# GpSimd issues two of the four transfers that bring a unit's probability blocks back

## What is computed

```python
xn = layernorm(x, ln_x_g, ln_x_b);  ln = layernorm(latents, ln_l_g, ln_l_b)
q = ln @ Wq
kv = concatenate([xn @ Wkv, ln @ Wkv], axis=1)
sim = einsum('bhid,bhjd->bhij', rmsnorm(q, qn_g) * scale, rmsnorm(k, kn_g))
attn = softmax(sim)                       # over 1024 context rows and 64 latents
out = einsum('bhij,bhjd->bhid', attn, v)  # then @ Wout + bout
```

## Time and profile before

| | |
|---|---|
| median of 3 runs | 220.82 us (219.22 to 222.07) |
| profiled execution | 220.61 us |
| its span | 218.8 us |
| TensorE's mean granted clock | 0.997 of full speed |
| busy: TensorE, weight loads, VectorE, ScalarE, GpSimd | 210.0, 179.2, 158.3, 142.1, 83.2 us |
| by the six stores (`p_spread<-xnh_room` and `<-xnl_room`) | 512 KB each |
| by the 24 read-backs | 128 KB each |

### The profile page before, as it was taken

How to read it: one execution, slowest core, us unless ns; L and a number is a source line. 1 busy time by engine, 2 the same in 40 slices (tenths; PEclk the granted TensorE clock), 3 DMA queues, 4 the chain that set the end, 5 groups by cost and what they waited for, 6 DMA issues and landing times.

```text
span 218.8 us, 4012 instructions
## 1 busy us (share of the span) xinstructions
PE 210.0 (96%) x1338; PEld 179.2 (82%) x1338; DVE 158.3 (72%) x355; ACT 142.1 (65%) x316; POOL 83.2 (38%) x135
## 2 busy tenths in 40 slices
PE   8899999999999999999999999999799999999984
PEld 7566878887787988889898988978588998899873
DVE  3799999998978989898886758876477651613531
ACT  3777798979985968776676595945566563315060
POOL 4388887872393939355160500012101200000400
PEclk9999999999999999999999999999999999999998
DMA  5491127110000232331514899435754580000000
GB/s 169 150 313 39 52 52 263 48 51 0 2 25 0 97 100 96 96 140 55 186 61 139 284 415 322 116 136 192 240 192 169 197 142 12 4 0 0 0 3 24
DMA packets 22820, 25.07 MB, mean 115 GB/s; under 512 B 7656, under 2 KB 20112, under 8 KB 22544
## 3 DMA queue, kind: packets, MB, share of 16 engines
q1 hardware_dynamic: 21384, 20.10, 29.6%
q0 software_dynamic: 864, 3.15, 3.7%
q10 hardware_dynamic: 552, 1.58, 2.1%
HBM read 18.65 MB, written 5.90 MB: 112 GB/s over the span
## 4 chain that ended last, share of the span: by engine, by line
PE 57%; DVE 13%; ACT 9%; issue 7%; DMA 6%; POOL 6%; SPq 1%; ACTq 0%; POOLq 0%; DVEq 0%
PE banks L1611 11%; PE banks L1505 8%; PE banks L1436 7%; PE banks L1545 6%; PE banks L1819 5%; PE banks L1661 3%; DVE small L1089 3%; DMA xnl_room<-p_spread 2%; DVE sk L1101 2%; DMA raw<-in_ctx 2%; PE banks L1625 2%; ACT sp L759 2%; PE banks L1626 2%; PE banks L1668 2%; PE banks L1548 2%
## 5 line engine op out<-in xcount | busy, mean ns | idle before, releaser
L607 POOL TENSOR_TENSOR small<-small 128x16 f32<-128x16 f32 x7 | 20.4, 2915 | 27.4 <-DVE small L1096 27.4
L720 ACT ACTIVATE sk<-banks 128x512 f32<-128x512 f32 x36 | 20.8, 602 | 11.7 <-PE banks L1505 11.1
L1089 DVE TENSOR_REDUCE small<-sk 128x8 f32<-128x512 f32 x36 | 23.5, 679 | 3.5 <-ACT sk L720 3.5
L1101 DVE TENSOR_TENSOR sk<-banks,small 128x512 f32<-128x512 f32 x36 | 23.0, 680 | 2.7 <-POOL small L607 2.4
L759 ACT ACTIVATE sp<-sp,small 128x1088 f32<-128x1088 f32 x16 | 19.2, 1203 | 7.4 <-DVE small L1120 6.9
L1611 PE MATMUL banks<-xnh,pth 128*128 128x256 f32 x80 | 23.6, 295 | 0.0
L1505 PE MATMUL banks<-wkh,xth 128*128 128x512 f32 x68 | 22.7, 415 | 0.6 <-ACT xth L700 0.5
L1611 PE MATMUL banks<-xnh,ptl 128*128 128x256 f32 x80 | 22.6, 283 | 0.0
L1611 PE MATMUL banks<-xnl,pth 128*128 128x256 f32 x80 | 22.6, 283 | 0.0
L1120 DVE CUSTOM_DVE_ANT_0 sp<-banks,mbias 128x1088 f32<-128x1088 f32 x16 | 20.5, 1284 | 2.0 <-PE banks L1548 2.0
L1505 PE MATMUL banks<-wkl,xth 128*128 128x512 f32 x68 | 21.4, 396 | 0.3 <-DVE wkl L1187 0.3
(11 more groups left out here) (227 smaller groups left out, 538.3 us busy)
## 6 DMA issues: line engine op xcount, KB each, us to landing
knT<-in_L_attn_qkv_kernel SPq DMA_DIRECT2D x1, 3072.0 KB, 12.1
spread<-knT SPq DMA_DIRECT2D x5, 512.0 KB, 2.6
knT<-spread SPq DMA_DIRECT2D x20, 128.0 KB, 2.9
raw<-in_ctx SPq DMA_DIRECT2D x16, 128.0 KB, 2.4
p_spread<-xnh_room POOLq DMA_DIRECT2D x3, 512.0 KB, 3.1
xnh_room<-p_spread SPq DMA_DIRECT2D x12, 128.0 KB, 2.8
p_spread<-xnl_room POOLq DMA_DIRECT2D x3, 512.0 KB, 3.4
xnl_room<-p_spread SPq DMA_DIRECT2D x12, 128.0 KB, 3.0
```

The costliest lines, as they stand in the source:

```text
L607: nc.gpsimd.tensor_tensor(rn[:, i % 2, :], n2[:, i % 2, :], mhalf, ALU.pow).then_inc(rnp_ready, 1)
L720: nc.scalar.activation(sk[:, i % 2, h * 512:(h + 1) * 512], banks[:, k_bank(i, h), :], ACT.Square).then_inc(sq_ready, 1)
L1089: mark(nc.vector.tensor_reduce(n2[:, i % 2, 8 * h:8 * h + 8], sk[:, i % 2, h * 512:(h + 1) * 512].rearrange("p (h d) -> p h d", d=DH), AX. ...
L1101: nc.vector.tensor_tensor(sk[:, i % 2, h * 512:(h + 1) * 512].rearrange("p (h d) -> p h d", d=DH), banks[:, k_bank(i, h), :].rearrange("p ...
```

## The change

SP issues the first two reads of each unit (rows 0 to 63 of `p_back`). The other two are issued by GpSimd, in `store_blocks(u)` behind the store of the same unit, after a wait for that store and, from n = 2, for `ptl_ready`, as SP has it. Each of GpSimd's twelve reads has a semaphore of its own, `pq_by_pool[n][c]`. ScalarE waits for both of them beside `pq_landed`, whose count per unit falls from 64 to 32. The lines behind the new line 296 are one further down (on ScalarE, nine to ten).

```diff
--- before.py
+++ after.py
@@ -293,6 +293,7 @@
         mh_ps = sem("mh_ps")
         ph_half = sem("ph_half")
         pb_stored = [sem(f"pb_stored{n}") for n in range(UNITS - SPREAD)]
+        pq_by_pool = [[sem(f"pq_by_pool{n}_{c}") for c in range(2)] for n in range(UNITS - SPREAD)]
         pq_landed = [sem("pq_landed0"), sem("pq_landed1")]
         qg_ready = sem("qg_ready")
         qbd_ready = sem("qbd_ready")
@@ -525,7 +526,7 @@
                 if n >= 2:
                     sp.wait_ge(ptl_ready, split_count(u - 2, 0))
 
-                for c in range(4):
+                for c in range(2):
                     sp.dma_start(p_back[n % 2][c * QD:(c + 1) * QD, :].rearrange("a (i m) -> a i m", i=4),
                                  p_spread[n][:, c * D:(c + 1) * D].rearrange("(i a) m -> a i m", i=4)
                                  ).then_inc(pq_landed[n % 2], 16)
@@ -646,10 +647,17 @@
                     nc.gpsimd.tensor_scalar(qg[:, 3:4], qg[:, 2:3], DH ** -0.5, 0.0, ALU.mult, ALU.add).then_inc(qg_ready, 1)
 
             def store_blocks(u):
-
                 n = u - SPREAD
+
                 pool.wait_ge(pb_ready, n + 1)
                 pool.dma_start(p_spread[n], p_blocks[n % 2]).then_inc(pb_stored[n], 16)
+                pool.wait_ge(pb_stored[n], 16)
+                if n >= 2:
+                    pool.wait_ge(ptl_ready, split_count(u - 2, 0))
+                for c in range(2, 4):
+                    pool.dma_start(p_back[n % 2][c * QD:(c + 1) * QD, :].rearrange("a (i m) -> a i m", i=4),
+                                   p_spread[n][:, c * D:(c + 1) * D].rearrange("(i a) m -> a i m", i=4)
+                                   ).then_inc(pq_by_pool[n][c - 2], 16)
 
             for u in range(ITEMS - ITEMS_A, UNITS):
                 latents_twice(u)
@@ -782,7 +790,9 @@
 
             def spread_high(u):
                 n = u - SPREAD
-                act.wait_ge(pq_landed[n % 2], 64 * (n // 2 + 1))
+                act.wait_ge(pq_landed[n % 2], 32 * (n // 2 + 1))
+                for c in range(2):
+                    act.wait_ge(pq_by_pool[n][c], 16)
                 if u == SPREAD:
                     act.wait_ge(u_ps, u)
```

## The result

The changed kernel took 222.94 us (median of 4 runs, 222.24 to 224.49) where the kernel before took 220.76 us beside it (4 runs, 219.22 to 222.07). The ratio is 1.011, 95% interval 1.007 to 1.016: **slower by 1.1%**. That is inside the 2% that the chances were made for, but the interval leaves out both the forecast of 219.2 and "no change". The profiled execution took 222.24 us with a span of 220.1, against 220.61 and 218.8.

What follows compares the result with a forecast made beforehand. TensorE, busy 210.0 of 218.8 us, was taken as the bound, with one transfer stall of 1.59 us at unit 11. Removing it gave 220.61 - 1.59 = 219.0, as a median 219.2 us, range 218.0 to 223.5.

Steps and rivals of the forecast that it cites:

- the 2% classes: Chances against a 2% (4.4 us) threshold: faster 0.01, within 0.92, slower 0.07.
- the stall at unit 11: TensorE idles 1.59 us before mix_high(11), for a last read-back landing after 5.00 us beside the next unit's store.
- (a): SP issues two reads per unit, not four, and is free some 0.86 us earlier; worth nothing by itself.
- the price c of a GpSimd read: GpSimd's own time for one read, taken as 0.53 us; gain turns to loss at about 0.75.
- rival C: GpSimd's turn, 4.0 + 2c (c: its time per read), becomes the bound: 0.5 to 4.9 us slower; chance 0.22.
- (d): GpSimd's added waits delay the latents' copy and next store, with 2 us or more in hand; nothing on the path.
- (e): ScalarE waits on three semaphores, not one, before its copy: nothing to 0.1 us a unit, taken as 0.
- (c): The next unit's store stands behind GpSimd's reads, at 153.1 not 151.76, so unit 11's reads escape contention.
- the sum's turn of 5.05 us: One GpSimd turn: copy 0.24, start 0.30, store to landing 3.1, start 0.30, two reads, some 0.05; all units in time.
- rival B: DMA engine sharing stays, last reads still take 5.0 us, only 0.5 us of issue saved: 220.3 us; chance 0.08.
- the landing of a read of GpSimd's: Each read-back issued by GpSimd was taken to land 2.9 us after issue.
- A: Unit 15's read meets Wout1's loads, or stores take 3.4 to 4.0 us: gain 0.3 to 1.3 us; chance 0.17.

Runs made afterwards that it cites:

- the first experiment: Kernel before, plus GpSimd's added waits but no reads on GpSimd (SP issues all four); also called the waits alone: 220.8 us, ratio 0.999.
- help for units 10 to 13: Changed kernel, but GpSimd issues two reads only for units 10 to 13; SP issues all four of units 14 and 15: 221.68 us, ratio 1.003.
- the half stores: Each store moves 256 KB, not 512; output not the reference's. On the changed kernel 219.34 us, ratio 0.993; on the kernel before 218.57 us, 0.990.
- three of four: Changed kernel, but GpSimd issues three of each unit's four reads and SP one: 224.34 us, ratio 1.019.
- the third experiment: Changed kernel, but SP waits for GpSimd's two reads of unit 15 before loading Wout1; also called Wout1 held back: 222.35 us, ratio 1.008.
- one of four: Changed kernel, but GpSimd issues one of each unit's four reads and SP three: 222.81 us, ratio 1.013.
- help for unit 11 alone: Changed kernel, but GpSimd waits and issues two reads only for unit 11; SP issues all four for the other five units: 221.1 us, ratio 1.000.
- two fillers: Kernel before, plus GpSimd's added waits and two unused additions in place of its reads; SP issues all four reads: 222.8 us, ratio 1.010.
- the store in two halves: Kernel before, but GpSimd stores each unit as two 256 KB transfers and SP starts two reads after the first half lands: 218.67 us, ratio 0.992.

## Why the prediction was wrong

**The forecast's direction was wrong**: 1.6 us of gain was forecast, 2.2 us of loss measured. Its time range (to 223.5) and the 2% classes held.

*What held.* The bound and the stall at unit 11 were read rightly: half the store's bytes take it away, in a kernel that is otherwise the one before. (a) and the price c of a GpSimd read were right, 0.55 us against 0.53, so rival C's condition on c did not come up. (The Trainium skill, SBUF — State Buffer, SBUF: two separate sides, has GpSimd blocked while VectorE holds the port pair that both share. No issue of the twelve reads took over 0.576 us, so none waited out one of VectorE's operations of 1.2 us.) (d) the waits cost nothing by themselves (the first experiment). (e) the three waits took 0.15 us from landing (174.13 + 4.42 = 178.55) to the copy (178.70) against 0.03 before, a little over the 0 to 0.1 allowed. The store of unit 12 was issued at 152.71 (forecast 153.1) and unit 11's stall went, in full.

*The step that failed* is (c), "that is the part that takes the contention away", and with it the term of 3.1 us for store to landing in the sum's turn of 5.05 us. The store was held back to the end of the reads' issue, not of their flight. The reads are in flight for some 3 us after it, and they meet the store in every unit. Before, unit 11's reads lost at such a meeting; the store took 3.98 us too, but it had left early enough. Now the store is the one that is late, and the store is the head of the next unit's chain: its reads wait for it. The four stores of units 12 to 15 took 4.0, 4.38, 3.85 and 3.73 us, 16.0 together, where the sum had 12.4. The turns were 5.54, 5.92 and 5.40 us and not 5.05. The instruction packet has a share in the 4.38, but where it came at another time, with help for units 10 to 13, the stores of units 12 to 14 still took 3.58, 3.69 and 3.97.

The warning was in the rows. The range of the stores' landings was 2.9 to 4.0, and a slow store was left to rival A as a chance of one term and not asked for its cause in each turn. And under rival B the prediction says that unit 12's reads had no store beside them. They had: the last was issued at 157.1 and the store of unit 13 at 157.33. The reads landed in 2.8 us all the same, and the store took 3.75 us and not 3.1. That is the arrangement of (c), a store right behind the reads, and its price fell on the store. A slip made the margin look wider still: by its own turn of 5.05 us the store of unit 15 lands at 171.35, not at 171.1, with 0.6 us in hand and not 0.8.

*The second term that was too small* is the landing of a read of GpSimd's, 2.9 us. Unit 10's, with no store beside them, took 3.4, and with the half stores the median was 3.5. It is not a price of GpSimd's queue as such, since with three of four they took 2.83 to 2.91 in that unit; it came there where two or three of SP's reads ran beside. That is 0.5 us more per unit, and perhaps most of the 0.8 us by which the helped form stays behind with half stores; this was not tested. In unit 15 the errors add up: the store landed at 173.30 (forecast 171.1) and the last read at 178.55 (forecast 174.9, wanted by 175.7), the latter with the instruction packet beside it (176.0 to 177.0 us), which no term of the sum had.

*The rivals.* A had the right sort of event, a late last read (4.42 us, within its 4.0 to 5.0), but its cause, Wout1, is refuted by the third experiment (the instruction packet stood in its place), and as a loss it was bounded at 1.3 us of a gain. B fell as a time: the reads of unit 11 did get faster, 3.7 us at most. Yet its reason was the sound one. The Trainium skill (DMA: Bandwidth & Descriptors, Issuing engines are not separate DMA queues) says that transfers of different engines interleave on the same DMA engines, so issuing from several saves only sequencer time. The runs agree in both directions: the stores moved to SP's queue landed as late (4.48, 4.55) as on GpSimd's. The prediction set that rule aside because the order of issue had changed; order only chose who was late. C's time is what came about, 222.9 where it had 223.5 at its middle, with the other reason: its own test was a turn longer than 5.5 us (c over 0.75), and the mean turn was 5.62, from the store's landing and not from c.

*What stays open.* How much of the loss is the meeting of reads and stores and how much the instruction packet. Half the store's bytes took away the stalls of both kernels but for 0.24 us, with the instruction packet there as in all others, so the packet alone makes no such loss. But the last read of unit 15 took 4.0 to 5.0 us in the changed kernel, with the waits alone, with Wout1 held back and with three and one of four, and in each of these the packet was under way with it. In the kernel before it came at 176.1, when that read was all but done, and the read took 3.14. It was also under way with the late reads of unit 12 with help for unit 11 alone and with two fillers, but with no late read of unit 11 before. No kernel moved the packet by intent. Nor is it shown how a read and a store divide a DMA engine, only that half the store's bytes is enough. The half stores keep about the mean size of a packet (queue q0 fell from 864 packets with 3.15 MB to 480 with 1.57 MB), so their size was not tested apart from their number.

## What to carry to other kernels

A transfer that is held back to protect another one still meets it if "back" means behind its issue and not behind its landing; ask which of the two is the head of the next step's chain, since that one can afford it less. Where a stall comes from a meeting of two transfers, moving the issue to another engine, or the order, passed the stall on here; fewer bytes or an earlier start of the one that is waited for (the store in two halves) took it away. Before a late landing is put down to a neighbour, look at the rows of the instruction queues for that stretch as well. In a loop in which each turn waits for the last, write the turn's sum with the landing times under the new overlap, and compare it with the period of the work that it must keep up with: here 0.6 us more in each turn turned a gain into a loss.

## What the runs showed of the hardware

The same 128 KB read-back is cut otherwise on the two queues. Twelve reads taken off queue q1 removed 1728 packets (21384 to 19656), 144 each; on queue q0 they added 576 (864 to 1440), 48 each. Fewer packets did not make them faster: 3.3 to 4.4 us to land against 2.5 to 3.6 for SP's in the same kernel, and 3.4 against 2.5 and 2.8 in unit 10, with no store beside them; the least that a read of GpSimd's took was 2.83, with one read of SP's ahead of it.

One packet of 16 KB with instructions held one DMA engine for 0.9 to 1.7 us, and a transfer with a share on that engine waited for it: with Wout1 held back, 30 of the read's 32 packets were moved by 177.0 us and the other two only behind the instruction packet, from 178.0. Two stalls of TensorE, of 2.01 and 2.06 us, were followed by 3.4 us at a granted clock of 0.50 (1.2 GHz; two fillers, and Wout1 held back); after one of 2.32 us (help for unit 11 alone) and one of 2.51 (three of four) it stayed at 1.00.

A DMA's wait until it lands depends on what is issued after it as well as before it. The store of unit 10, with no read-back near it, took 3.1 to 3.2 us to land (2.6 from SP's queue), and full stores issued at most 0.8 us behind the last of a unit's reads took 3.2 to 5.2 us, on either queue. Where a store was issued in the middle of four reads the last of them took 4.0 to 5.3 us; where it was issued 0.3 to 0.5 us behind the last one, on either queue and with no instruction packet beside it, that read took 2.5 to 3.2, and quiet ones took 2.5 to 2.9. The Trainium skill (DMA: Bandwidth & Descriptors, Queues, rings and completion order) says that each DMA engine goes round the queues that have work for it, a packet at a time. The late reads with a store in their middle agree with that; the late stores behind reads on SP's one queue (4.48 and 4.55 us) are no such turn-taking between queues, and no run here separates the two.
